# Sixteen places for expert weights, seven of them in the room of the MLP's weights, which are decoded from the eighth expert group on

## What is computed

```python
# layer 0: a state-space block, then 64 experts, 8 of them for each token, 64 rows per expert
x = x + ga * mamba(h)
xin = zeros((64, 64 + 1, 256)).at[eid, slot].set(h[tok])
hid = silu(xin @ wg) * (xin @ wu)          # wg, wu: 64 x 256 x 96
out = hid @ wd                             # wd: 64 x 96 x 256
x = x + gb * sum_over_8(out[eid, slot] * w)
# layer 1: attention with a window of 64, then an MLP of 2048 with 4-bit weights
x = x + ga * (attention(h) @ out_w1 @ out_w2)
Wg, Wu, Wd = dequant_nvfp4(packed, scales)
x = x + gb * ((gelu(h @ Wg.T) * (h @ Wu.T)) @ Wd.T)
```

## Time and profile before

| what | value |
|---|---|
| median of 3 runs | 689.96 us (688.8 to 691.51) |
| profiled execution: its own time | 693.05 us |
| profiled execution: span | 691.4 us |
| mean granted TensorE clock | 0.937 of full |
| PE busy in the span | 605.3 us (88%) |
| expert groups, first gather matmul to last down matmul | 177.67 to 299.6 us |
| attention and MLP | from 339 us (first `rotate`) to the end |

### The profile page before, as it was taken

The page is one execution under the profiler, slowest core; times in us unless marked ns, Lnnn a source line. Parts: engine busy times, 40 slices in busy tenths (PEclk is TensorE's granted clock), DMA queues, the critical chain, the costliest instruction groups (busy, mean ns, idle before and its releaser), DMA issues.

```text
span 691.4 us, 10308 instructions
## 1 busy us (share of the span) xinstructions
PE 605.3 (88%) x3516; PEld 471.9 (68%) x3516; DVE 461.5 (67%) x985; ACT 316.8 (46%) x967; POOL 165.3 (24%) x228
## 2 busy tenths in 40 slices
PE   2999899984798899885579999999998899989995
PEld 0554577763786788654356777787776788878885
DVE  5847667653599899735577877987576456653444
ACT  1674356442233223210478989999977211111110
POOL 1225701101001011127773243000004256500000
PEclk9999999995799899958588999999999999999999
DMA  8200151200044899973331452300000000000000
GB/s 311 83 1 0 35 177 32 67 1 1 1 165 128 234 259 305 288 256 99 91 97 33 47 60 36 29 1 2 1 1 0 1 1 1 0 31 1 1 0 31
DMA packets 23363, 50.35 MB, mean 73 GB/s; under 512 B 5520, under 2 KB 8720, under 8 KB 22800
## 3 DMA queue, kind: packets, MB, share of 16 engines
q1 hardware_dynamic: 18960, 37.10, 17.5%
q0 software_dynamic: 4352, 12.59, 8.9%
HBM read 44.43 MB, written 5.24 MB: 72 GB/s over the span
## 4 chain that ended last, share of the span: by engine, by line
PE 54%; DVE 18%; ACT 11%; issue 7%; SPq 5%; DMA 3%; POOL 2%; POOLq 0%; ACTq 0%; DVEq 0%
PE bank L1800 13%; PE bank L1776 7%; ACT arena L731 3%; PE bank L1290 3%; PE bank L1428 2%; PE bank L1446 2%; DVE spot L1024 2%; PE bank L1417 2%; PE bank L1674 2%; PE bank L1619 2%; ACT arena L756 2%; PE bank L1284 2%; SPq L320 1%; SPq L315 1%; ACT arena L702 1%
## 5 line engine op out<-in xcount | busy, mean ns | idle before, releaser
L1446 PE MATMUL bank<-spot,h_hi 128*128 128x256 f32 x256 | 66.8, 299 | 9.3 <-DVE spot L1024 9.1
L837 ACT ACTIVATE arena<-bank 128x512 f32<-128x512 f32 x32 | 19.2, 599 | 115.8 <-PE bank L1800 115.8
L1446 PE MATMUL bank<-spot,h 128*128 128x256 f32 x256 | 65.0, 292 | 0.0
L1261 DVE TENSOR_TENSOR arena<-arena,bank 128x512 f32<-128x512 f32 x32 | 22.0, 687 | 60.4 <-ACT arena L837 60.4
L1446 PEld LDWEIGHTS bank<-spot,h_hi 128*128 128x128 f32 x256 | 51.3, 201 | 15.0 <-DVE spot L1024 10.5
L438 POOL TENSOR_TENSOR low<-arena,gu_hi 128x128 fp32r<-128x128 f32 x56 | 26.0, 494 | 124.1 <-DVE dn_hi L1210 124.1
L1446 PEld LDWEIGHTS bank<-spot,h 128*128 128x128 f32 x256 | 51.3, 200 | 0.0
L1800 PE MATMUL bank<-h_hi,low 128*128 128x512 f32 x128 | 50.4, 394 | 0.0
L568 ACT ACTIVATE arena<-bank,arena 128x256 f32<-128x256 f32 x32 | 16.3, 560 | 68.2 <-PE bank L1446 68.2
L1800 PE MATMUL bank<-h_hi,gu_hi 128*128 128x512 f32 x112 | 44.9, 401 | 1.8 <-issue 0.9
L1800 PE MATMUL bank<-h_low,gu_hi 128*128 128x512 f32 x112 | 44.6, 398 | 0.0
(11 more groups left out here) (307 smaller groups left out, 1654.4 us busy)
## 6 DMA issues: line engine op xcount, KB each, us to landing
arena<-in_wgu SPq DMA_DIRECT2D x32, 384.0 KB, 4.4
arena<-in_wd SPq DMA_DIRECT2D x32, 192.0 KB, 5.3
expert_out<-arena POOLq DMA_DIRECT2D x16, 256.0 KB, 5.3
arena<-in_w SPq DMA_DIRECT2D x1, 2048.0 KB, 9.5
arena<-in_wmod SPq DMA_DIRECT2D x1, 1536.0 KB, 14.9
arena<-in_w_in SPq DMA_DIRECT2D x1, 1288.0 KB, 8.7
arena<-in_x SPq DMA_DIRECT2D x1, 1024.0 KB, 5.6
arena<-in_wmod SPq DMA_DIRECT2D x1, 1024.0 KB, 11.8
```

The source lines that it names most:

```text
L837: act.activation(gl[n % 3], bank[2 * (n % 3)][:, :], ACT.Gelu_apprx_tanh).then_inc(gl_ready, 1)
L1261: link(dve.tensor_tensor(it[n % 3], gl[n % 3], bank[2 * (n % 3) + 1][:, :], ALU.mult))
L1446: ins = pe.matmul(bank[g % 2][:, 2 * P * j:2 * P * (j + 1)], rounded(part[:, j * P:(j + 1) * P]), rounded(spot[g % 2][:, t, :]), start=t = ...
```

## The change

The nine places stay, in another order, and seven more places (`once_at`) are laid into the room where the decoded MLP weights will stand; pairs 9 to 15 use them once. They are loaded before the groups begin. Pairs 16 to 31 go round the nine places. Decoding now starts in group 7: `HALVES` says how many halves VectorE does behind each group's `hid`: 2, 1, 2, 1, 2, 1, 2 in groups 7 to 13, then 4 in group 14, 4 in group 15, and the last 5 behind the loop. Each decode waits for the groups that used the room. `load_codes` of chunks 0 and 1 is issued before the groups; that of chunk n (2 to 11) stands in SP's list behind the pairs of the group in which chunk n-2 is finished: chunk 2 in group 7, 3 in 9, 4 in 10, 5 in 11, 6 in 13, 7 and 8 in 14, 9 and 10 in 15, 11 behind the loop. The attention's weights stay at the end of group 13's turn, so the codes of chunks 7 to 11 come behind them. The decode's scratch shrinks from three tiles to two, and the code buffers move by 256. `keys(0)`, `values(0)` and `scores_a(0)` get waits on the decoding or the padding, and the padding of the keys is written between the gathers of tiles 1 and 2.

```diff
-        NS = 9
+        NB, NS = 9, 16
+        base_at = [X0 + PAIR, X0, A0 + 3 * PAIR, X0 + 2 * PAIR, X0 + 3 * PAIR, A0, A0 + PAIR, A0 + 4 * PAIR, A0 + 2 * PAIR]
+        once_at = [A0 + 11520, A0 + 15488, A0 + 16976, A0 + 18256, A0 + 20176, A0 + 21456, A0 + 22736]
+        slot_at = base_at + once_at
+        slot_of = [q if q < NS else (q - NS) % NB for q in range(E // 2)]
+        last_in = [q - NS if q < NS + NB else q - NB for q in range(E // 2)]
+        times_in = [1 if q < NS else 2 + (q - NS) // NB for q in range(E // 2)]
...
+        HALVES = [0] * 7 + [2, 1, 2, 1, 2, 1, 2, 4, 4]
+        done_at = [next((g for g in range(NG) if sum(HALVES[:g + 1]) >= 2 * n + 2), NG) for n in range(NQ)]
...
-                i = q % NS
+                i = slot_of[q]
                 if q >= NS:
-                    sp.wait_ge(down_mm, (q - NS) // 2 + 1)
+                    sp.wait_ge(down_mm, last_in[q] // 2 + 1)
...
+            sp.wait_ge(Yo_mm, T - 1)
+            for q in (NB, NB + 2, NB + 3):
                 load_pair(q)
+            sp.wait_ge(y_ready, T)
+            for q in (NB + 4, NB + 5, NB + 6):
+                load_pair(q)
+            sp.wait_ge(o_mm, T)
+            load_pair(NB + 1)
+            load_codes(0)
+            load_codes(1)
             for g in range(NG):
-                while n < NQ and n <= g - 1:
-                    load_codes(n)
-                    n += 1
-                for q in (2 * g + NS - 1, 2 * g + NS):
-                    if NS <= q < E // 2:
+                for q in range(NS, E // 2):
+                    if last_in[q] // 2 == g:
                         load_pair(q)
+                for n in range(2, NQ):
+                    if done_at[n - 2] == g:
+                        load_codes(n)
                 if g == 13:
                     sp.wait_ge(down_mm, 14)
...
+            for n in range(2, NQ):
+                if done_at[n - 2] == NG:
+                    load_codes(n)
...
             for t in range(T):
                 gather_first(t)
                 gather_rest(t)
+                if t == 1:
+                    pool.wait_ge(dec_done, NQ)
+                    pool.memset(kT[:, 0:WIN], 0.0).then_inc(pads, 1)
...
             def decode(n, par):
                 which, c, b = n // 4, n % 4, n % 2
+                dve.wait_ge(down_mm, 6 + min(which, 2))
                 dve.wait_ge(pk_loaded[b], DEC_LOADS[n])
...
-                while late < 2 * NQ and late < 2 * (g - 3):
-                    decode(late // 2, late % 2)
-                    late += 1
+                for half in range(late, late + HALVES[g]):
+                    decode(half // 2, half % 2)
+                late += HALVES[g]
+            for half in range(late, 2 * NQ):
+                decode(half // 2, half % 2)
             dve.wait_ge(cols3_mm, 1)
...
-                    pe.wait_ge(w_loaded[q % NS], 32 * (q // NS + 1))
+                    pe.wait_ge(w_loaded[slot_of[q]], 32 * times_in[q])
```

More of the change, by code:

```diff
@@ L146, in adaln_two_layers @@
         yT_mm, yT_ready, o_mm, x1_ready = map(sem, ["yT_mm", "yT_ready", "o_mm", "x1_ready"])
-        NS = 9
+        NB, NS = 9, 16
         PAIR = 4 * KC * FI + 2 * DM
-        slot_at = [X0 + PAIR * (i + 1) if i < 3 else A0 + PAIR * (i - 3) if i < 6 else X0 if i == 6 else A0 + PAIR * (i - 4) for i in range(NS)]
+        base_at = [X0 + PAIR, X0, A0 + 3 * PAIR, X0 + 2 * PAIR, X0 + 3 * PAIR, A0, A0 + PAIR, A0 + 4 * PAIR, A0 + 2 * PAIR]
[4 more added lines that the diff above has]
+        times_in = [1 if q < NS else 2 + (q - NS) // NB for q in range(E // 2)]
         wgu_s = [at(o, 2, 2 * KC * FI) for o in slot_at]
@@ L193, in adaln_two_layers @@
         D0 = A0 + 23808
-        pk = [at(D0 + 512 * i, QC) for i in range(2)]
-        sc = [at(D0 + 1024 + 512 * i, QC) for i in range(2)]
-        nib = [[at(D0 + 2048 + 256 * (3 * b + i), QC // 2) for i in range(3)] for b in range(2)]
+        pk = [at(D0 + 256 + 512 * i, QC) for i in range(2)]
+        sc = [at(D0 + 1280 + 512 * i, QC) for i in range(2)]
+        nib = [[at(D0 + 2304 + 256 * (2 * b + i), QC // 2) for i in range(2)] for b in range(2)]
         NQ = 3 * MLP // QC
-        NEARLY, PACE = 0, 1.5
+        HALVES = [0] * 7 + [2, 1, 2, 1, 2, 1, 2, 4, 4]
+        done_at = [next((g for g in range(NG) if sum(HALVES[:g + 1]) >= 2 * n + 2), NG) for n in range(NQ)]
         DEC_LOADS = [144 * len(range(n % 2, n + 1, 2)) for n in range(NQ)]
@@ L321, in load_codes @@
                                      blocks[r:r + 1, 2 * c:2 * c + 2, :].to_broadcast([16, 2, DM])).then_inc(pk_loaded[i], 16)
-            for q, tile, early in ((0, 1, True), (1, 2, True), (2, 2, True), (3, 3, True), (6, 3, True), (4, 1, False),
-                                   (5, 2, False), (7, 4, False), (8, 5, False)):
-                sp.wait_ge(st_mm if early else yT_mm, tile)
-                load_pair(q)
-            sp.wait_ge(yT_mm, T)
-            for n in range(NEARLY):
-                load_codes(n)
-            n = NEARLY
-            for g in range(NG):
-                while n < NQ and n <= g - 1:
-                    load_codes(n)
-                    n += 1
-                for q in (2 * g + NS - 1, 2 * g + NS):
-                    if NS <= q < E // 2:
+            sp.wait_ge(st_mm, 1)
+            load_pair(0)
+            sp.wait_ge(st_mm, 2)
+            load_pair(3)
+            load_pair(4)
+            sp.wait_ge(st_mm, 3)
+            load_pair(5)
+            load_pair(1)
+            sp.wait_ge(yT_mm, 1)
+            load_pair(6)
+            sp.wait_ge(yT_mm, 2)
+            load_pair(8)
+            sp.wait_ge(yT_mm, 4)
+            load_pair(2)
+            sp.wait_ge(yT_mm, 5)
+            load_pair(7)
+            sp.wait_ge(Yo_mm, T - 1)
+            for q in (NB, NB + 2, NB + 3):
+                load_pair(q)
+            sp.wait_ge(y_ready, T)
[5 more added lines that the diff above has]
+            load_codes(1)
+            for g in range(NG):
+                for q in range(NS, E // 2):
+                    if last_in[q] // 2 == g:
                         load_pair(q)
+                for n in range(2, NQ):
+                    if done_at[n - 2] == g:
+                        load_codes(n)
                 if g == 13:
@@ L409, in _ @@
             pool.wait_ge(down_mm, NG)
-            pool.memset(kT[:, 0:WIN], 0.0).then_inc(pads, 1)
             pool.memset(V_mix[0], 0.0).then_inc(pads, 1)
@@ L632, in keys @@
             def keys(t):
+                if t == 0:
+                    act.wait_ge(dec_done, NQ)
                 act.wait_ge(kv_mm, t + 1)
@@ L716, in values @@
             def values(t):
+                if t == 0:
+                    act.wait_ge(pads, 1)
                 act.wait_ge(kv_mm, t + 1)
@@ L1054, in decode @@
                 which, c, b = n // 4, n % 4, n % 2
+                dve.wait_ge(down_mm, 6 + min(which, 2))
                 dve.wait_ge(pk_loaded[b], DEC_LOADS[n])
                 codes = pk[b].bitcast(i16).rearrange("p (n two) -> p n two", two=2)[:, :, 0]
-                v, f, s = (nib[b][i].bitcast(i16) for i in range(3))
-                ff = nib[b][1].bitcast(f16)
+                v, s = (nib[b][i].bitcast(i16) for i in range(2))
+                ff = nib[b][0].bitcast(f16)
                 if par == 0:
@@ L1065, in decode @@
                     link(dve.tensor_scalar(s, codes, 0x80, 8, ALU.bitwise_and, ALU.logical_shift_left))
-                link(dve.tensor_tensor(f, v, s, ALU.bitwise_or))
+                link(dve.tensor_tensor(v, v, s, ALU.bitwise_or))
                 if which < 2:
@@ L1077, in decode @@
                     last.then_inc(dec_done, 1)
[L1079 to L1082, removed]
+            late = 0
             for g in range(NG):
@@ L1455, in gate_up @@
                     q = 2 * g + i
-                    pe.wait_ge(w_loaded[q % NS], 32 * (q // NS + 1))
+                    pe.wait_ge(w_loaded[slot_of[q]], 32 * times_in[q])
                     for j in range(KC):
                         for e in range(2):
-                            w = wgu_s[q % NS][:, e, :].rearrange("p (a j f) -> p a j f", a=2, j=KC)
+                            w = wgu_s[slot_of[q]][:, e, :].rearrange("p (a j f) -> p a j f", a=2, j=KC)
                             ins = pe.matmul(bank[2 + g % 2][64 * e:64 * e + CAP, 2 * FI * i:2 * FI * (i + 1)],
@@ L1478, in down @@
                         ins = pe.matmul(bank[6 + g % 2][64 * e:64 * e + CAP, i * DM:(i + 1) * DM],
-                                 hidT[g % 2][:, i * P + 64 * e:i * P + 64 * e + CAP], wd_s[(2 * g + i) % NS][:, e, :])
+                                 hidT[g % 2][:, i * P + 64 * e:i * P + 64 * e + CAP], wd_s[slot_of[2 * g + i]][:, e, :])
                 ins.then_inc(down_mm, 1)
@@ L1612, in scores_a @@
                 pe.wait_ge(qcT_ready, min(t + 2, T))
+                if t == 0:
+                    pe.wait_ge(pads, 6)
                 own = kT[:, WIN + t * P:WIN + t * P + 64]
```

1 line of the change is left out of this document (removed).

## The result

The changed kernel takes 711.5 us (median, 708.04 to 712.26), the one before, run on the same chip, 690.74: ratio 1.0295, 95% interval 1.0252 to 1.0338. It is slower, as forecast, but by 20.8 us instead of 13.3, and lies 2.5 us above the upper end of the range. The profiled execution took 708.04 with a span of 706.2, so it is the lowest of the four.

What follows compares the result with a forecast made beforehand. TensorE is busy 88% of the span, so only its waits can give time. 6.2 us gained in group 5, 2.2 lost at chunk 3 and late decoding in the tail move rotate(0) by +13.3: 703 us, range 694 to 709.

Steps and rivals of the forecast that it cites:

- the gain in group 5: Expert group 5: without a chunk to decode there, the period falls from 13.19 to about 7.0, 6.2 us gained.
- the end of the decoding in place of the gather: Attention's start: decoding ends at 325.7 and decides it, no longer the last gather; rotate(0) moves by +13.3 us.
- the 2.2 us at chunk 3: Chunk 3's codes, issued behind pairs 27 and 28, are ready at 271.2, wanted at 269.1: 2.2 us lost, the middle estimate.
- the landing of chunk 7's codes at 299.9: Tail: chunk 7's codes queue behind the attention's 3.9 MB, drained at 298.4, and land at 299.9; hid(15) comes at 301.8.
- the far end of this term: Chunk 3, worst case: 3.6 us lost with a 4.6 us landing, plus 2.5 if the clock falls.
- Chunks 7 to 11, from the start of 7: Tail: chunks 9 to 11 each wait for a buffer and then codes, so decoding ends at 325.7.
- the product: Output matrices' product, from end of decoding to combine(0): 11.2 us, ends 9.1 and 12.
- rotate(0) at 352.4: Attention's start: rotate(0) follows when tile 0's queries are copied, at 352.4 instead of 339.07, +13.3 us.
- The base: Whole time: +13.3 us on the profiled 693.05 gives 706.4; on the median of 689.96 it gives 703.
- The third: Rival: stall at chunk 3 lowers the clock, landings of 4.6 us at chunks 3, 9 and 11; +20, 710 us; chance 0.11.
- Overtaking: Rival: chunk 7's codes overtake the attention's big loads and land at 295.5; +8.9, 699 us; chance 0.2.
- hidden decoding: Rival: between hid(14) and the attention, codes are always there and decoding stays hidden; faster, 679.5 us; chance 0.07.

Runs made afterwards that it cites:

- act_queue: Changed kernel with the attention's 3.9 MB of weights issued from ScalarE's list instead of SP's; 707.68 us, ratio 1.0255.
- weights_last: Changed kernel with the attention's 3.9 MB of weights moved behind the last codes in SP's list; 713.57 us, ratio 1.0349.
- second profile: Profile of a repeat run of the changed kernel, unaltered; 711.78 us, ratio 1.031 against the kernel before.
- early_hid: Changed kernel with 3 half chunks instead of 4 decoded behind hid(14); 714.43 us, ratio 1.0332.
- act_rows: Changed kernel with the attention's weights issued from ScalarE's list, the two large matrices as 12 transfers with 2 KB rows; 710.5 us, ratio 1.0266.

## Why the forecast was short

The direction held, and most of the mechanism: the gain in group 5, the codes behind pairs at chunk 3, the attention's weights ahead of chunk 7's codes, and the end of the decoding in place of the gather as what sets the attention's start. What failed is the size of two terms, the 2.2 us at chunk 3 (5.2 measured) and the landing of chunk 7's codes at 299.9 (3.4 later beyond that), and a wait ahead of rotate(0) that the sum did not have (1.2). The reason given for chunk 7's wait, the order in the queue, held only in part. Measured from the first gather in the profiled pair, the forecast's points and what came:

| point | forecast | measured | lag |
|---|---|---|---|
| hid(14) | 106.3 | 109.3 | +3.0 |
| chunk 7 begins | 122.2 | 128.6 | +6.3 |
| decoding ends | 148.0 | 153.4 | +5.4 |
| combine(0) | 159.2 | 163.6 | +4.3 |
| rotate(0) | 174.7 | 180.2 | +5.5 |

*Group 5: right.* 6.2 us forecast, 13.19 - 6.89 = 6.3 measured.

*"2.2 us lost" at chunk 3: 5.2 measured.* down(9) ended when forecast: SP's issue behind it starts 78.3 us after the first gather, forecast 78.3. Then four pair DMAs took 2.4 us instead of 1.9, and the codes landed 4.1 after the last issue instead of 3.2. That makes a wait of 3.74, and the slow clock behind it 1.5. I had both the 4.6 us landing and the clock as the far end of this term and took the middle row; codes that follow four transfers of weights are nearer to the far end.

*"299.9" for chunk 7: 3.4 us late beyond that.* Relative to hid(14) I had the big loads drained at 14.4 us and the codes 1.5 behind them, at the same bytes per us. wqup landed at about 15.7, and the codes 3.6 behind. The price by bytes was too low for these nine DMAs: 3.6 us for 0.5 MB instead of 1.5. Their own issue had slowed to 7.58 us, but what made up the 3.6 us is not shown. The rule of the Trainium skill cited with the forecast (DMA: Bandwidth & Descriptors, Queues, rings and completion order), ring order within a queue, agrees with these 3.6 us: the codes did not overtake. But the queue's order, which the forecast gave as the reason, was not the cause by itself: with no big load in their own queue the codes of act_queue were used only 1.9 us sooner. Most of the wait is for the 3.9 MB in flight, on their own queue or another: without them chunk 7 began 8.2 us after hid(14) (weights_last).

*Chunks 7 to 11, from the start of 7, and the product* were each 1 us shorter than forecast: 24.8 instead of 25.8, and 10.2 instead of 11.2. These two errors the other way hid 2 us of the lag.

*"rotate(0) at 352.4": a wait that I did not have, +1.2.* In the changed kernel combine(1) follows norm_a(0) without a wait, and norm_a of tile 1 waits 4.06 us for its root in ScalarE's list, which stands behind the four query copies of tile 0. Before, the gather held tile 1 back further than that the earlier trace rows. The forecast let rotate(0) start at the end of the copies, although in the old trace it starts 2.1 us after them (339.07 against 336.95), behind norm_a(1) in VectorE's list.

*The base.* I put the sum on the median as if both kernels' executions differed by it alone. They do not: in whole time the profiled pair differs by 15.0 us only, because the changed kernel's groups began 2.6 us earlier and what follows rotate(0) took 1.4 less; from the first gather to rotate(0) it loses 18.8. The second profile loses 20.9 there, 1.1 more at hid(14), behind chunk 3, and 1.3 more in the product. Of the 7.5 us missing in the forecast, about 5.5 are the terms above. The other 2 agree with what the second profile loses more, but beside starts that vary by 2.9 us that share is an estimate.

*The rivals.* The third, clock down at chunk 3 with slow landings, 710 us at a chance of 0.11, is nearest to what happened; its first term, 6.1 us of landing and clock at chunk 3, was nearer to the 5.2 measured, but it put slow landings at chunks 9 and 11, where they were shorter than forecast. Overtaking and hidden decoding are out. The range ended at 709 because it left out the far end of that case.

## What to carry to other kernels

Before small loads are put near a large one, ask what drains beside them, not only what stands ahead in their own list: another queue gained 1.9 us at chunk 7, taking the bytes away 11.1, and then the bytes' own user waited. The longest wait in a profile need not cost anything: early_hid took 15 us off it without gain, because another chain ended later. When one new stall idles TensorE, price the slow clock with it and take the landing from rows that lie behind other transfers.

## What the runs showed that I had not expected

Chunk 7's codes, eight loads of 32 KB and one of 256 KB, were used 8.2 us after hid(14) without the 3.9 MB, 19.3 behind them on the same queue, 17.5 beside them on another queue with rows of up to 16 KB, and 12.3 with rows of 2 KB, whose issue was also spread over 11.1 us instead of 4.5.

SP's issue was slower with more in flight: the same nine issues took 4.5 us without the 3.9 MB (289.31 to 293.76 in weights_last), 4.6 beside them on the other queue in rows of 2 KB (act_rows), 5.4 beside them there in rows of up to 16 KB (act_queue), and 7.6 behind them on SP's own.

The granted clock averaged 0.72 over the six us behind 3.74 us of idle TensorE, and stayed at 1.00 where the idle time was 0.29 us (215:226) and, in act_queue, where it was 3.02 us (270:276).

The first gather matmul stands between 175.07 and 177.96 us in the profiles looked at, whatever the kernel. Its cause was not looked for and stays open.
